# Routing table, first stage and q/k/v projections of a one-core transformer block: unrolled, re-tiled and re-shared among the engines

## The reference

```python
x = x + 0.5 * ffn(layernorm(x), gate_weight, gate_up_proj, down_proj, similarity_matrix)
x = x + attn(layernorm(x), W_dq, W_uq, W_dkv, W_uk, W_uv, W_o)
x = x + 0.5 * ffn(layernorm(x), gate_weight, gate_up_proj, down_proj, similarity_matrix)
```

## Time and profile before

| | |
|---|---|
| time, median of 3 runs | 1367.84 us (1364.95 to 1369.25) |
| the profiled execution | 1371.37 us, span of its records 1369.6 us |
| mean granted TensorE clock | 0.883 |
| busy: PE, DVE, ACT, POOL | 1097.5 (80%), 852.2 (62%), 669.7 (49%), 450.8 us (33%) |
| `al` | 8.8 to 61.6 us |
| `ar` | 61.6 to 107.7 us |
| `q` | 333.2 to 456.5 us |
| `bl`, `br` | 986 to 1056.1, 1056.1 to 1102.1 us |

### The profile page before, as it was taken

The page is one execution under the profiler, slowest core; times in us unless marked ns, Lnnn a source line. Parts: engine busy times, 40 slices in busy tenths (PEclk is TensorE's granted clock), DMA queues, the critical chain, the costliest instruction groups (busy, mean ns, idle before and its releaser), DMA issues. The chain is left out here.

```text
span 1369.6 us, 23532 instructions
## 1 busy us (share of the span) xinstructions
PE 1097.5 (80%) x7116; PEld 664.2 (48%) x7116; DVE 852.2 (62%) x2534; ACT 669.7 (49%) x1676; POOL 450.8 (33%) x456
## 2 busy tenths in 40 slices
PE   2548988884787599999999999999687489888850
PEld 1336777774343134444444444443265367777740
DVE  4774333332885688888888888886066733333327
ACT  2513444442466047677666766666556134344420
POOL 3635666663244400000000000000057356666630
PEclk8557999998688579999999999999898579999985
DMA  7602222223645903345554344340176022222239
GB/s 227 222 0 67 88 90 89 89 87 129 214 151 151 156 4 56 57 68 70 69 71 56 56 56 56 57 56 18 42 220 186 0 62 86 93 85 90 89 107 316
DMA packets 109439, 133.03 MB, mean 97 GB/s; under 512 B 30032, under 2 KB 83728, under 8 KB 109328
## 3 DMA queue, kind: packets, MB, share of 16 engines
q1 hardware_dynamic: 91280, 89.65, 29.3%
q0 software_dynamic: 13824, 37.77, 8.7%
q10 hardware_dynamic: 4224, 4.19, 0.9%
HBM read 82.68 MB, written 48.50 MB: 96 GB/s over the span
## 5 line engine op out<-in xcount | busy, mean ns | idle before, releaser
L1363 ACT ACTIVATE t_prob<-t_psS 128x512 f32<-128x512 f32 (+3 forms) x768 | 326.4, 495 | 173.4 <-PE t_psS L1295 149.2
L1383 DVE CUSTOM_DVE_ANT_0 t_psR<-t_psR,all_causal 128x128 f32<-128x128 f32 (+3 forms) x512 | 245.4, 504 | 48.3 <-PE t_psR L1273 44.7
L1273 PE MATMUL t_psR<-stacks_kst,stacks_qst 96*128 96x512 bf16 (+3 forms) x768 | 231.0, 345 | 24.2 <-PEq L851 16.3
L1292 PE MATMUL t_psS<-stacks_qst,stacks_kst 99*128 99x512 bf16 (+3 forms) x768 | 224.0, 332 | 2.2 <-ACT t_prob L1363 1.5
L1387 DVE TENSOR_REDUCE t_maxp<-t_psR 128x1 f32<-128x512 f32 x256 | 175.5, 686 | 23.2 <-PE t_psR L1273 22.7
L1306 PE MATMUL t_psO<-t_prob,t_vst 128*32 128x512 f32 (+3 forms) x1536 | 163.8, 498 | 3.0 <-ACT t_prob L1363 1.1
L1273 PEld LDWEIGHTS t_psR<-stacks_kst,stacks_qst 96*128 96x128 bf16 x768 | 70.1, 98 | 196.4 <-DVE t_maxp L1383 95.0
L1263 POOL COPY t_vst<-stacks_values 128x512 f32<-128x512 f32 x16 | 9.8, 615 | 423.8 <-DMA stacks_kst<-qk_parts 423.5
L644 PE MATMUL be_psG<-b_w,be_xT 128*128 x432 | 116.2, 405 | 10.2 <-issue 6.6
L644 PE MATMUL ae_psG<-a_w,ae_xT 128*128 x432 | 115.0, 402 | 10.3 <-issue 8.0
L1295 PE MATMUL t_psS<-all_causal_t,all_ident_bf 128*128 128x128 bf16 x512 | 109.6, 221 | 0.0
(11 more groups left out here) (286 smaller groups left out, 1892.5 us busy)
## 6 DMA issues: line engine op xcount, KB each, us to landing
qk_parts<-q_parts SPq DMA_DIRECT2D x32, 384.0 KB, 2.6
stacks_qst<-qk_parts SPq DMA_DIRECT2D x96, 128.0 KB, 4.8
stacks_kst<-qk_parts SPq DMA_DIRECT2D x96, 128.0 KB, 7.7
q_yk<-y_rows SPq DMA_DIRECT2D x16, 512.0 KB, 5.9
s_yk<-y_rows SPq DMA_DIRECT2D x16, 512.0 KB, 9.9
o_rows<-t_orow SPq DMA_DIRECT2D x32, 136.0 KB, 8.9
bl_raw<-o_rows SPq DMA_DIRECT2D x8, 544.0 KB, 3.8
xn_rows<-al_xn SPq DMA_DIRECT2D x8, 512.0 KB, 4.1
```

Source lines behind the costliest of these rows:

```text
L1273: nc.tensor.matmul(psR[bank][:, 0:w], qst[slot][0:KROWS, h, i * P:(i + 1) * P], kst[slot][0:KROWS, h, k0:k0 + w], start=True, stop=True).t ...
L1292: ins = nc.tensor.matmul(ps, kst[k][0:MROWS, h, j * P:(j + 1) * P], qst[k][0:MROWS, h, a:(c + 1) * 512], start=True, stop=a > j * P)
L1363: nc.scalar.activation(prob[j % 2][:, h, a:(c + 1) * 512], psS[n % ST_BANKS][:, a - c * 512:512], ACT.Exp, scale=DK ** -0.5).then_inc(exp_ ...
L1383: ins = nc.vector.tensor_tensor_reduce(psR[bank][:, 0:w], psR[bank][:, 0:w], T.causal[:, 512 - w:512], 1.0, -BIG, ALU.add, ALU.max, maxp[: ...
```

## The change

It touches five places.

1. The constants are no longer a block: `T.make` runs them on POOL at the head of `al`, `const_ready` is waited for before the first deviation, and SP issues the first x before the gate. There are some other constants.
2. `al`, `bl` and `q` have no loop any more: all steps are written out.
3. The weights of an expert are fetched two steps earlier, and ACT and POOL treat all eight within `al` (and `bl`).
4. The routing table: DVE multiplies `tile_hot` by one f16 number itself (`tile_number`, a number from 1 to 2048), PE has 8 matmuls a round, which add into four groups of PSUM columns, and DVE adds the start of the group behind it. ACT and POOL take no part.
5. `q`: the projections come in the order q0 k0 q1 k1 (`TURN`), DVE does the first add and the statistics ahead of `left`, and ACT normalises the rows.

The diff, cut to its core:

```diff
-            for c in range(-2, 2):
-                step(c, c % 2, has(c))
-            with eng.Fori(1, CH // 2 - 1) as it:
-                for b in range(2):
-                    step(it * 2 + b, b, has(it))
-            for c in range(CH - 2, CH + 2):
-                step(c, c % 2, has(c))
+        def steps(step):
+            for c in range(-2, CH + 2):
+                step(c, c % 2, lambda d: 0 <= c + d < CH)
...
-                    hold(sp, xn_ready, c * U + U, T)
-                    sp.dma_start(xn_view[:, bass.ds(c * U, U), :], xn[:, b]).then_inc(xn_stored[b], 16)
+                    sp.wait_ge(xn_ready, c * U + U)
+                    sp.dma_start(xn_view[:, c * U:(c + 1) * U, :], xn[:, b]).then_inc(xn_stored[b], 16)
                     if loads and b == 0 and has(4):
                         loads(sp, c // 2 + 2)
-                    W.load(sp, c, b)
-                    if loads and isinstance(c, int) and c == CH - 2:
-                        load_others(sp)
+                if has(2):
+                    W.load(sp, c + 2, b)
+                if loads and c == CH - 2:
+                    load_others(sp)
...
-                if has(-2) and has(W.ROUTED - 2):
-                    W.low(pool, c - 2)
-            steps(pool, step)
+                if has(0):
+                    W.low(pool, c)
+            if loads:
+                T.make(pool)
...
+                    if loads and c == 0:
+                        act.wait_ge(T.const_ready, T.N_CONST)
                     ln.deviation(act, c)
-                if has(-2) and has(W.ROUTED - 2):
-                    W.high(act, c - 2, b)
-            steps(act, step)
+                if has(0):
+                    W.high(act, c, b)
...
-            for e in range(E - W.ROUTED, E):
-                W.high(act, e, e % 2)
...
-            c.link(v.memset(zeros[:], 0.0))
...
-            def hot(r, b):
-                cols = bass.ds(r * CW, CW)
+            def hot(r):
+                b, cols = r % 2, slice(r * CW, (r + 1) * CW)
                 lanes, tiles_of = [P, P, CW], [P, MT, CW]
                 wait(dve, hot_used, r - 1)
-                v.tensor_tensor(tile_hot[:, b], number16[:, 0:MT], bc(tile[:, cols], 1, tiles_of),
-                                ALU.is_equal).then_inc(hot_ready, 1)
-                v.tensor_tensor(lane_hot[:, b], number16[:], bc(lane[:, cols], 1, lanes),
-                                ALU.is_equal).then_inc(hot_ready, 1)
+                v.tensor_tensor(tile_hot[:, b], number16[:, 0:MT], bc(tile[:, cols], 1, tiles_of), ALU.is_equal).then_inc(hot_ready, 1)
+                v.tensor_tensor(lane_hot[:, b], number16[:], bc(lane[:, cols], 1, lanes), ALU.is_equal).then_inc(hot_ready, 1)
+                dve.wait_ge(hot_ready, r * 3 + 1)
+                v.tensor_tensor(tile_number[:, b], tile_hot[:, b], bc(T.number[:, cols], 1, tiles_of), ALU.mult).then_inc(hot_ready, 1)
             dve.wait_ge(exp_ready, 2)
-            table_steps(dve, hot)
-            te = [P, MT, E]
-            c.link(v.tensor_tensor(ended[:], bc(T.iota[:, 0:MT], 2, te), bc(tiles_end[:], 1, te), ALU.is_ge))
-            c.link(v.tensor_reduce(expert_f[:], ended[:], AX_X, ALU.add))
-            c.link(v.scalar_tensor_tensor(digits[:].rearrange("p i s -> p (i s)"), expert_f[0:1, :], float(E - 1),
-                                          T.digit[:].rearrange("p i s -> p (i s)"), ALU.min, ALU.mult))
-            c.link(v.tensor_reduce(word_f[:], digits[:], AX_X, ALU.add))
-            c.link(v.tensor_copy(R.experts[:], word_f[:]))
-            dve.wait_ge(table_done, 1)
-            found = ps_table[:, 0:MT]
-            c.link(v.scalar_tensor_tensor(empty[:], found, 0.0, T.unused_row[:], ALU.is_equal, ALU.mult))
-            c.link(v.scalar_tensor_tensor(R.slot[:], found, -1.0, empty[:], ALU.add, ALU.add))
+            for r in range(SLOTC // CW):
+                hot(r)
+                if r == 0:
+                    v.tensor_scalar(ended[:], tiles_end[:, 0:E - 1], T.lane_number[:], None, ALU.is_lt).then_inc(expert_ready, 1)
+                if r == 1:
+                    dve.wait_ge(expert_ready, 1)
+                    v.tensor_reduce(expert_f[:], ended[:], AX_X, ALU.add).then_inc(expert_ready, 1)
+            dve.wait_ge(packed, 1)
+            c.link(v.tensor_copy(R.experts[:], ps_count[0:1, 0:ITS]))
+            dve.wait_ge(hot_used, SLOTC // CW)
+            table = ps_table[:, 0:GROUPS * MT].rearrange("p (g t) -> p g t", g=GROUPS)
+            by_group = [P, GROUPS, MT]
+            c.link(v.scalar_tensor_tensor(begun[:], table, 0.0, bc(T.group_start[:], 2, by_group), ALU.is_gt, ALU.mult))
+            c.link(v.tensor_tensor(counted_from[:], begun[:], table, ALU.add))
+            c.link(v.tensor_reduce(found[:], counted_from[:].rearrange("p g t -> p t g"), AX_X, ALU.add))
+            c.link(v.scalar_tensor_tensor(empty[:], found[:], 0.0, T.unused_row[:], ALU.is_equal, ALU.mult))
+            c.link(v.scalar_tensor_tensor(R.slot[:], found[:], -1.0, empty[:], ALU.add, ALU.add))
...
-        @block.gpsimd
-        def _(pool):
-            def by_column(r, b):
-                cols = bass.ds(r * CW, CW)
-                hold(pool, hot_ready, r * 2 + 1, T)
-                hold(pool, hot_used, r - 1, T)
-                nc.gpsimd.tensor_tensor(tile_col[:, b], tile_hot[:, b], bc(T.col_number[:, cols], 1, [P, MT, CW]),
-                                        ALU.mult).then_inc(col_ready, 1)
-            for e in range(E - W.ROUTED, E):
-                W.low(pool, e)
-            table_steps(pool, by_column)
...
-            pe.wait_ge(hot_ready, 2)
-            nc.tensor.matmul(ps_table[:, 0:MT], lane_hot[:, 0, :, 0], zeros[:], start=True, stop=False)
-            def add(r, b):
-                pe.wait_ge(hot_ready, r * 2 + 2)
-                pe.wait_ge(col_ready, r + 1)
-                pe.wait_ge(number_ready, r + 1)
+            def add(r):
+                pe.wait_ge(hot_ready, r * 3 + 3)
                 for j in range(CW):
-                    for number in (tile_col, tile_lane):
-                        ins = nc.tensor.matmul(ps_table[:, 0:MT], lane_hot[:, b, :, j], number[:, b, :, j], start=False, stop=False)
+                    col = r * CW + j
+                    g, at = col // GCOLS, col % GCOLS
+                    ins = nc.tensor.matmul(ps_table[:, g * MT:(g + 1) * MT], lane_hot[:, r % 2, :, j], tile_number[:, r % 2, :, j],
+                                           start=(at == 0), stop=(at == GCOLS - 1))
                 ins.then_inc(hot_used, 1)
-            table_steps(pe, add)
-            nc.tensor.matmul(ps_table[:, 0:MT], lane_hot[:, 1, :, 0], zeros[:], start=False, stop=True).then_inc(table_done, 1)
+            for r in range(SLOTC // CW):
+                add(r)
+                if r == 2:
+                    pe.wait_ge(expert_ready, 2)
+                    nc.tensor.matmul(ps_count[0:1, 0:ITS], expert_f[0:MT, :], T.pack[0:MT, :], start=True, stop=True).then_inc(packed, 1)
...
+    def shifts(self, dve):
+        self.nc.vector.scalar_tensor_tensor(self.shift[:], self.moments[:, :, 0], -1.0, self.rstd[:],
+                                            ALU.mult, ALU.mult).then_inc(self.shift_ready, 1)
+    def normalised_by_act(self, s, out, rows):
+        return self.nc.scalar.activation(out, rows, ACT.Identity, scale=self.rstd[:, s:s + 1], bias=self.shift[:, s:s + 1])
...
+        TURN = (0, 2, 1, 3)
...
                 for s in range(U):
-                    if now:
-                        r = c * NU + s
-                        dve.wait_ge(high_ready, r + 1)
-                        wait(dve, low_ready, r - 1)
-                        nc.vector.tensor_tensor(left[:, s % 2, :], psU[s % 2][:], parts[:, s, 0, :], ALU.subtract).then_inc(left_ready, 1)
                     if ahead:
-                        weight = [R.weight[:, k, bass.ds(a * U + s, 1)] for k in range(TOPK)]
+                        weight = [R.weight[:, k, a * U + s:a * U + s + 1] for k in range(TOPK)]
                         if s == 0:
                             dve.wait_ge(T.y_loaded[a % Y_BUFS], (a // Y_BUFS + 1) * 16 * TOPK)
                         nc.vector.scalar_tensor_tensor(row(a, s), yk[:, a % Y_BUFS, 0, s, :], weight[0], row(a, s),
                                                        ALU.mult, ALU.add).then_inc(first_added, 1)
                         if s:
                             stats(s - 1)
+                    if now:
+                        r = c * NU + s
+                        dve.wait_ge(high_ready, r + 1)
+                        wait(dve, low_ready, r - 1)
+                        nc.vector.tensor_tensor(left[:, s % 2, :], psU[s % 2][:], parts[:, TURN[s], 0, :],
+                                                ALU.subtract).then_inc(left_ready, 1)
+                    if ahead:
                         dve.wait_ge(first_added, a * U + s + 1)
```

(32 more changed lines are left out.)

181 lines of the change are left out of this document (81 added, 100 removed).

## The result

The changed kernel took 1353.78 us (median of 4, 1350.82 to 1355.32) against 1366.39 us of before (median of 4), a ratio of 0.990 (95% interval 0.988 to 0.993). It is faster by 13 us, where 40.5 were forecast; 1353.78 lies outside the range.

| stage | before | after | moved | forecast |
|---|---|---|---|---|
| start and `al` | 61.6 | 62.0 | +0.4 | -11.5 |
| `ar` | 46.1 | 33.8 | -12.3 | -12.3 |
| `ae` | 225.5 | 226.6 | +1.1 | 0 |
| `q` | 155.4 | 163.9 | +8.5 | -2 |
| attention | 497.4 | 496.8 | -0.6 | 0 |

What follows compares the result with a forecast made beforehand. It took DMA to bound the first stage, DVE routing and fast q/k/v steps, PE slow ones. Terms -11.5 - 24.6 - 2.4 - 2.0 = -40.5 from the median 1367.84 gave 1327.3, predicted as 1327.5 us, range 1316 to 1340.

Steps and rivals of the forecast that it cites:

- a round of 1.4: Routing table: a round becomes DVE work alone, 1.38 us, eight of them 11.1 us.
- -12.3 forecast: Each routing stage: 12.3 us less (bounds -10 and -13.5), -24.6 for both.
- Rival 3: Routing table not bound by DVE: PE's matmuls and hand-over stay, 2.2 us a round, 1340.5 in all; chance 0.06.
- Rival 4: Written-out steps: instruction fetches come late, slower than before, 1379 us with twelve uncovered fetches; chance 0.02.
- Two more roundings and two more subtractions lie inside the stage ... so they fit in idle time: First stage: roundings of 1.47 us and subtractions of 7.8 or less fit POOL's and ACT's idle time, except the last.
- The term of -11.5: First stage: transfers start 7.8 us earlier with a deeper queue, stage ends at 50.1; bounds -7 and -14.
- rival 1: First stage gives only its shift, turned rows waiting behind weight roundings on ACT: -5, 1334 us; chance 0.18.
- a DMA share of 0.93: First stage: with a deeper queue the 14.5 MB need 48.7 us, from 1.0 to 49.7; share before 0.87.
- rival 2: q/k/v gets slower: ACT's longer chain delays the turn, all eight steps at the low level, +5, 1334.5 us; chance 0.20.
- if it stays near the 1.32 of the earlier trace the slow steps vanish: q/k/v: with PE's idle time before the turn near 1.32 us, eight steps of 11.5 instead of mean 12.3 give -6.
- The forecast of -2: q/k/v stage: 2 us less, range -5 to +5; +2 to +3 if every second step stays slow.
- not 0.6: `bl`: four steps leave the loop, each saving 0.6 us, -2.4 in all (0 to -3).

Runs made afterwards that it cites:

- const_block: Changed kernel with the constants back in a block of their own ahead of everything: 1303.51 us against 1295.03 of the changed kernel; first stage ended at 67.9.
- best_dve: Changed kernel with q/k/v normalisation on VectorE and, in the first stage alone, GpSimd's subtraction in four pieces, one step later: 1273.84 us, 0.970 of before.
- best_split: As `best_dve`, but two of the four q/k/v normalisations on ScalarE: 1278.3 us, 0.974 of before.

## Why the prediction was right and wrong

**Routing: right, in mechanism and size.** Four rows at 0.42, a round of 1.4, tail of 2.4 us: -12.3 forecast, -12.3 measured, twice. Rival 3 fell. One reading in it was wrong without harm: the rows of `tile_hot` are not 0.46 throughout. One of the eight of before took 1.54 us, from 0.44 us behind the start of GpSimd's product at 85.99; it was inside the 22.25 us that the sum started from.

```profile
86.43 1.54 DVE L513 TENSOR_TENSOR ar_tile_hot<-ar_number,ar_tile 128x576 f16<-128x576 f16 x1
```

Rival 4 fell too: the page of the changed kernel has 63 transfers of instructions where that of before has 62, and the written-out steps of `bl` are the shorter ones.

**First stage: the step that failed** is "Two more roundings and two more subtractions lie inside the stage ... so they fit in idle time". GpSimd's own time was free, but its instructions hold VectorE's normalisation, which had gone from 17.6 to 26.0 us. The earlier trace rows showed the price, 1.9 for 0.42 us, and the prediction used it for the routing, where the work leaves, and not for the stage where it arrives. The slow groups were in the trace of before, too (5.38, 3.37 and 1.99 us for four normalisations); they were not looked for. The term of -11.5 came out at +0.4. Shown by runs, against 58.2 to 62.0: without GpSimd's work 52.6, with pieces 54.5 to 56.5, with the work of two experts back in the routing and all of it two steps later 52.5. Beside it rival 1 was at work: ScalarE stands 5.25 us in front of a rounding, and one step's delay on top of the pieces gave 3 us (56.4 to 53.4). The early start itself was not the error (`const_block`, 6 to 10 us). The other part of the term, a DMA share of 0.93, was never reached: 0.77 in the changed kernel and 0.88 in `best_dve`, whose first stage ends at 52.3 and not at 50.1; and the bytes are 61.23 us x 251 GB/s = 15.4 MB, not 14.5, since the window of the earlier trace rows left out the stage's end.

**q/k/v: rival 2 in size, its mechanism in part.** The forecast's step that failed is "if it stays near the 1.32 of the earlier trace rows the slow steps vanish": the idle time ahead of the turn was 1.66 to 2.13 us in every step. The mechanism was in the text ("queued behind the normalisations on ACT is the first rounding of the next step"), but it was priced at +0.3 a step against a gain that never came. ScalarE's price was taken from copies out of PSUM, 0.4 us an operation; from SBUF with scale and bias it is 0.585, 0.49 to 0.51 between starts, so 2.07 for four and beyond the bound of 2.0. VectorE's first add covers 0.5 of the 2.8 us between its product and its subtraction. And the slow steps did not vanish: PE's granted clock was at 1.00 in one step and between 0.62 and 0.74 in the others shown. The step at 1.00 (397.42 to 409.71) took 12.3 us, where such a step took 11.2 before: that 1.1 us is the chain through ScalarE. The steps at a lower clock take 13.0 to 14.1, and there are more of them; rival 2 had this part. How the 9.2 us by which the stage grew divide between the two is not shown. The forecast of -2 was +8.5; giving the normalisation back took 10.0 us off the stage (115.9 to 105.9), more than it had grown by.

**bl: mechanism right, size off.** A step in the loop costs 0.3 us more than one outside, not 0.6 (6.9 against 7.2; the last steps of the earlier trace rows are shorter for another reason, since 6.60 stands outside the loop in both kernels). Four steps make -1.2 us, where the transfers are on time.

**The sum.** What was forecast is nearly what the mended kernel gives: 1314.64 to 1273.84 is -40.8. That its parts are the forecast's is not shown, since its q/k/v stage gave more than -2 and its first stage less than -11.5 (52.3 is -9.3). Open: why the q/k/v stage ends on a slow step in some executions and on a fast one in others, what `best_split` loses, and `ae`, `be` and `s`, whose changes of 1 to 2 us were not looked into.
